# Where the diagonal blocks of B are built in a four-layer sequence kernel with a two-way state-space layer

## The reference, cut to what matters

```python
dbc = einsum('bse,re->bsr', u, Wdbc)
dlt, Bm, Cm = split(dbc, [R, R + N], axis=-1)          # R = 64, N = 16
delta = softplus(einsum('bsr,er->bse', dlt, Wdt) + bdt)
dA = exp(delta[..., None] * A)
dBu = delta[..., None] * Bm[:, :, None, :] * u[..., None]
h = dA_t * h + dBu_t                                    # per time step
y = einsum('ben,bn->be', h, C_t)
```

## Time and profile before

| what | value |
|---|---|
| median of 3 runs | 6139.45 us (6117.95 to 6150.0) |
| profiled execution | 6128.12 us, span 6126.3 us |
| input pass | about 2757 to 3141 us of the span |
| scans | about 3141 to the end |
| PE busy | 5604.4 us, 91% |
| DVE busy | 4365.8 us, 71% |
| ACT busy | 2988.3 us, 49% |
| POOL busy | 2959.0 us, 48% |
| mean granted TensorE clock | 0.977 of full speed |

### The profile page before, as it was taken

One profiled execution on the slowest core, in us unless ns is written; L12 is line 12 of the kernel. 1 busy time (PEld: TensorE's weight loads), 2 busy tenths in 40 slices (PEclk: granted clock), 3 DMA queues, 4 the chain that ended last, 5 costly groups with the idle time before them and its releaser, 6 DMA issues. The chain is left out here.

```text
span 6126.3 us, 136499 instructions
## 1 busy us (share of the span) xinstructions
PE 5604.4 (91%) x58464; PEld 3147.5 (51%) x58464; DVE 4365.8 (71%) x5868; ACT 2988.3 (49%) x4999; POOL 2959.0 (48%) x953
## 2 busy tenths in 40 slices
PE   8899979997999989977989999999999999999998
PEld 2455545554455545543445555555555555555555
DVE  1165545554455555557549999999999999999996
ACT  0022212221455555551137666666666666666664
POOL 0000100000000000004349989899899998989997
PEclk9999989998999999988999999999999999999999
DMA  5200120001000000004431101111111111101110
GB/s 209 80 16 31 38 73 16 31 33 59 18 8 17 22 20 17 8 15 156 154 122 47 61 19 57 60 56 61 41 50 50 57 64 50 65 23 57 62 47 31
DMA packets 142972, 321.72 MB, mean 53 GB/s; under 512 B 25769, under 2 KB 27050, under 8 KB 132154
## 3 DMA queue, kind: packets, MB, share of 16 engines
q1 hardware_dynamic: 142402, 313.39, 14.7%
HBM read 238.46 MB, written 74.89 MB: 51 GB/s over the span
## 5 line engine op out<-in xcount | busy, mean ns | idle before, releaser
L1847 POOL TENSOR_TENSOR sc_state<-sc_state,sc_c_rows 128x2048 f32<-128x2048 f32 x512 | 2374.6, 4643 | 282.6 <-DVE sc_state L2154 268.2
L2154 DVE TENSOR_TENSOR_SCAN sc_state<-sc_decay,wide 128x512 f32<-128x512 f32 x2048 | 2346.4, 1200 | 100.1 <-PE wide L2013 95.5
L1938 ACT ACTIVATE sc_decay<-sc_delta,sc_neg_a 128x512 f32<-128x512 f32 x2048 | 1455.6, 720 | 813.2 <-DVE sc_state L2154 808.4
L2013 PEld LDWEIGHTS wide<-sc_diag,sc_du_t 64*64 64x64 f32 x32768 | 971.4, 133 | 688.1 <-issue 450.8
L2013 PE MATMUL wide<-sc_diag,sc_du_t 64*64 64x128 f32 x32768 | 1172.4, 273 | 136.6 <-DVE sc_state L2154 136.6
L2030 PE MATMUL wide<-sc_state,sc_half 64*64 64x512 f32 x8192 | 1077.1, 592 | 11.4 <-POOL sc_state L1847 11.4
L1328 DVE CUSTOM_DVE_ANT_0 l_prob<-wide,l_mask_add 128x512 f32<-128x512 f32 x512 | 340.1, 683 | 286.8 <-PE wide L1198 286.8
L1987 PE MATMUL wide<-sc_xn_t,sc_w_z 128*128 128x512 f32 x1024 | 510.0, 621 | 1.2 <-DMA sc_xn_t<-xn_d 1.2
L1113 ACT ACTIVATE l_prob<-l_prob,l_s_max 128x512 f32<-128x512 f32 x512 | 366.1, 716 | 229.3 <-DVE l_s_max L1328 228.9
L460 PE MATMUL wide<-l_w,l_xn_t 128*128 128x512 f32 x1024 | 445.1, 592 | 1.7 <-PEq L84 1.7
L1209 PE MATMUL wide<-l_ident,l_prob 128*128 128x128 f32 x2048 | 293.6, 281 | 65.3 <-DVE l_prob_t L1337 38.2
(11 more groups left out here) (197 smaller groups left out, 6605.0 us busy)
## 6 DMA issues: line engine op xcount, KB each, us to landing
sc_c_rows<-c_d SPq DMA_DIRECT2D x64, 1024.0 KB, 4.8
sc_w_z<-wz_tiles SPq DMA_DIRECT2D x128, 256.0 KB, 2.7
x<-l_out SPq DMA_DIRECT2D x24, 1024.0 KB, 4.2
l_x<-x SPq DMA_DIRECT2D x16, 1024.0 KB, 5.9
mx_d<-fr_mx SPq DMA_DIRECT2D x16, 1024.0 KB, 4.2
sc_mx<-mx_d SPq DMA_DIRECT2D x64, 256.0 KB, 2.7
pro_w_mod<-in_mod_w SPq DMA_DIRECT2D x6, 2048.0 KB, 8.4
l_w<-in_att_w SPq DMA_DIRECT2D x12, 1024.0 KB, 11.9
```

The costliest lines, as they stand in the source:

```text
L1847: pool.tensor_tensor(state[quad % STATES][:, :, :], state[quad % STATES][:, :, :], c_rows[(r * 4 + q) % ROWS][:, :, :], ALU.mult).then_inc ...
L1938: act.activation(decay[step % DECAYS][:, :], delta[slot % 2][:, :], ACT.Exp, scale=neg_a[:, s, m, n:n + 1]).then_inc(decay_ready, 1)
L2013: last = pe.matmul(to[cols_to, k, :, :], du_t[slot % 2][rows, k, cols_to], diag[rows, c, k, :, :], start=True, stop=True)
L2154: dve.tensor_tensor_scan(state[quad % STATES][:, step % 4, order], decay[step % DECAYS][:, order], pair[:, i, order], 0.0, ALU.mult, ALU.a ...
```

## The change

In the input pass the B product takes its time steps with a stride of four, so that b_tm already has the layout which the scans want, and b_tm has two buffers. GpSimd builds the diagonals of both sweeps there, into two buffers of 16 KB per partition, one for each sweep. Its builds of batch b stand in later iterations: the forward ones after the residual of batch b+1, the backward ones after the first 1/sqrt of batch b+2. SP stores them (2 MB for each sweep) to diag_d at the end of the iteration of the following batch. b_d is gone. In the scans GpSimd builds nothing; SP loads the eight chunks of `diag` (256 KB each) one by one as TensorE finishes with the old ones, and TensorE waits on one semaphore per chunk.

```diff
@@ front_layer @@
+        b_tm = [sb(f"b_tm{j}", [P, TT, 2, N]) for j in two]
+        half = sb("half", [P, 64])
+        diag = [sb(f"diag{s}", [P, 8, 4, 64, 2]) for s in two]
+                def store_diag(b, s):
+                    sp.wait_ge(diag_built[s], 8 * (b + 1))
+                    sp.dma_start(d["diag_d"][b, s], diag[s][:, :, :, :, :].rearrange("p c k j n -> p (c k j n)")
+                                 ).then_inc(diag_stored[s], 16)
...
-                    sp.wait_ge(b_drained, b + 1)
-                    sp.dma_start(d["b_d"][b].rearrange("(t p) n -> p t n", p=P),
-                                 b_tm[:, :, :, :].rearrange("p t s n -> p t (s n)")).then_inc(b_stored, 16)
                     for h in range(2):
                         sp.wait_ge(mx_ready, b * ET + h * 4 + 4)
                         sp.dma_start(d["mx_d"][b, h * 4:(h + 1) * 4].rearrange("m p t -> p m t"),
                                      mx[:, h * 4:(h + 1) * 4, :]).then_inc(mx_stored, 16)
+                    if b >= 1:
+                        for s in range(2):
+                            store_diag(b - 1, s)
+                for s in range(2):
+                    store_diag(B - 1, s)
...
+                def build(b, s):
+                    if b == 0:
+                        pool.wait_ge(half_loaded, 16)
+                    pool.wait_ge(b_drained, b + 1)
+                    if b >= 1:
+                        pool.wait_ge(diag_stored[s], b * 16)
+                    for c in range(8):
+                        pool.tensor_tensor(diag[s][:, c, :, :, :],
+                                           b_tm[b % 2][:, :, s, 2 * c:2 * c + 2].unsqueeze(2).broadcast_to([P, 4, 64, 2]),
+                                           half[:, :].unsqueeze(1).unsqueeze(3).broadcast_to([P, 4, 64, 2]), ALU.mult
+                                           ).then_inc(diag_built[s], 1)
                 for b in range(B):
                     rsqrt(b, mv, rstd, mv_ready, var_ready, rstd_ready)
+                    if b >= 2:
+                        build(b - 2, 1)
                     rsqrt(b, mv2, rstd2, mv2_ready, var2_ready, rstd2_ready)
                     residual(b)
+                    if b >= 1:
+                        build(b - 1, 0)
+                build(B - 2, 1)
+                build(B - 1, 0)
+                build(B - 1, 1)
...
-                                             xn_t[j][:, k, t * P:(t + 1) * P], w_dbc[:, :, k, R + N:R + 2 * N],
+                                             xn_t[j][:, k, t::4], w_dbc[:, :, k, R + N:R + 2 * N],
...
-                    if b >= 1:
-                        dve.wait_ge(b_stored, b * 16)
+                    if b >= 2:
+                        dve.wait_ge(diag_built[0], 8 * (b - 1))
+                        dve.wait_ge(diag_built[1], 8 * (b - 1))
@@ scan_layer @@
+                def load_diag(r, c):
+                    sp.dma_start(diag[:, c, :, :, :].rearrange("p k j n -> p (k j n)"),
+                                 d["diag_d"][r // 2, r % 2][:, c * 512:(c + 1) * 512]).then_inc(diag_loaded[c], 16)
...
                 load_xn(0)
+                for c in range(8):
+                    load_diag(0, c)
                 for quad in range(4):
                     load_c(quad)
...
                     if m == 7 and r + 1 < 2 * B:
-                        for q in range(1, 4):
-                            sp.wait_ge(weighted, 4 * slot + q)
-                            load_c(4 * (r + 1) + q)
+                        for c in range(8):
+                            sp.wait_ge(dbu_full, 4 * (8 * slot + c + 1))
+                            load_diag(r + 1, c)
+                            if c in (5, 7):
+                                q = (c - 3) // 2
+                                sp.wait_ge(weighted, 4 * slot + q)
+                                load_c(4 * (r + 1) + q)
+                        sp.wait_ge(weighted, 4 * slot + 3)
+                        load_c(4 * (r + 1) + 3)
...
-                    if m == 7 and r + 1 < 2 * B:
-                        build(r + 1, 2 * q)
-                        build(r + 1, 2 * q + 1)
...
-                        pe.wait_ge(diag_ready, r * 8 + c + 1)
+                        pe.wait_ge(diag_loaded[c], (r + 1) * 16)
```

More of the change, by code:

```diff
@@ L1412, in front_layer @@
         dbc = [sb(f"dbc{s}", [R + N, T]) for s in two]
-        b_tm = sb("b_tm", [P, TT, 2, N])
+        b_tm = [sb(f"b_tm{j}", [P, TT, 2, N]) for j in two]
+        half = sb("half", [P, 64])
+        diag = [sb(f"diag{s}", [P, 8, 4, 64, 2]) for s in two]
         stats = sb("stats", [P, TT, 6])
@@ L1430, in front_layer @@
         xn_stored, mx_stored, resid_stored = sem("xn_stored"), sem("mx_stored"), sem("resid_stored")
-        dbc_stored, b_stored = sem("dbc_stored"), sem("b_stored")
+        dbc_stored, half_loaded = sem("dbc_stored"), sem("half_loaded")
+        diag_built, diag_stored = [sem(f"diag_built{s}") for s in two], [sem(f"diag_stored{s}") for s in two]
         with nc.Block() as block:
@@ L1453, in _ @@
                 sp.dma_start(wx[:, :, :], d["wxT"].rearrange("(k p) n -> p k n", p=P)).then_inc(wx_loaded, 16)
+                sp.dma_start(half[:, :], d["half_ident"]).then_inc(half_loaded, 16)
                 load(1)
+                def store_diag(b, s):
+                    sp.wait_ge(diag_built[s], 8 * (b + 1))
+                    sp.dma_start(d["diag_d"][b, s], diag[s][:, :, :, :, :].rearrange("p c k j n -> p (c k j n)")
+                                 ).then_inc(diag_stored[s], 16)
                 for b in range(B):
@@ L1477, in _ @@
                 sp.wait_ge(dbc_stored, B * 64)
-                sp.wait_ge(b_stored, B * 16)
+                for s in range(2):
+                    sp.wait_ge(diag_stored[s], B * 16)
                 sp.wait_ge(mx_stored, B * 32)
@@ L1582, in drains @@
                     dve.wait_ge(b_full, b + 1)
-                    if b >= 1:
-                        dve.wait_ge(b_stored, b * 16)
-                    dve.tensor_tensor(b_tm[:, :, :, :], banks[4][:, 0:TT * 32].rearrange("p (t s n) -> p t s n", t=TT, s=2),
+                    if b >= 2:
+                        dve.wait_ge(diag_built[0], 8 * (b - 1))
+                        dve.wait_ge(diag_built[1], 8 * (b - 1))
+                    dve.tensor_tensor(b_tm[b % 2][:, :, :, :], banks[4][:, 0:TT * 32].rearrange("p (t s n) -> p t s n", t=TT, s=2),
                                       b_bias[:, :, R + N:R + 2 * N].unsqueeze(1).broadcast_to([P, TT, 2, N]), ALU.add
@@ L1655, in scan_layer @@
         dlt = [sb(f"dlt{i}", [P, T]) for i in two]
-        b_tm = [sb(f"b_tm{i}", [P, 4, N]) for i in two]
         diag = sb("diag", [P, 8, 4, 64, 2])
@@ L1681, in scan_layer @@
         w_z_loaded = [sem(f"w_z_loaded{i}") for i in range(WZ)]
-        dlt_loaded, b_loaded = [sem(f"dlt_loaded{i}") for i in two], [sem(f"b_loaded{i}") for i in two]
+        dlt_loaded, diag_loaded = [sem(f"dlt_loaded{i}") for i in two], [sem(f"diag_loaded{c}") for c in range(8)]
         c_loaded = [sem(f"c_loaded{i}") for i in range(ROWS)]
@@ L1685, in scan_layer @@
         gate_loaded, out_stored = sem("gate_loaded"), [sem(f"out_stored{i}") for i in two]
-        diag_ready, dl_full, soft_ready, delta_ready = sem("diag_ready"), sem("dl_full"), sem("soft_ready"), sem("delta_ready")
+        dl_full, soft_ready, delta_ready = sem("dl_full"), sem("soft_ready"), sem("delta_ready")
         z_full, z_direct, du_ready, turned, du_t_ready = sem("z_full"), sem("z_direct"), sem("du_ready"), sem("turned"), sem("du_t_ready")
@@ L1707, in load_set @@
                         sp.dma_start(dlt[r % 2][i * R:(i + 1) * R, :], d["dlt_d"][b, s]).then_inc(dlt_loaded[r % 2], 16)
-                        sp.dma_start(b_tm[r % 2][i * 64:(i + 1) * 64, :, :],
-                                     d["b_d"][b, i * 256:(i + 1) * 256, s * N:(s + 1) * N].rearrange("(j k) n -> j k n", k=4)
-                                     ).then_inc(b_loaded[r % 2], 16)
+                def load_diag(r, c):
+                    sp.dma_start(diag[:, c, :, :, :].rearrange("p k j n -> p (k j n)"),
+                                 d["diag_d"][r // 2, r % 2][:, c * 512:(c + 1) * 512]).then_inc(diag_loaded[c], 16)
                 def load_c(quad):
@@ L1754, in _ @@
                             sp.wait_ge(dl_full, 16 * r)
-                            sp.wait_ge(diag_ready, 8 * r)
                         load_set(r + 1)
@@ L1806, in _ @@
                 pool.wait_ge(const_loaded, 4 * 16)
[L1808 to L1817, removed]
                 def gating(slot):
@@ L1835, in output @@
                                        ).then_inc(out_ready, 1)
-                for c in range(8):
-                    build(0, c)
                 for quad in range(QUADS):
@@ L2190, in program @@
                             ("resid_d", [B, T, D]), ("xn_d", [B, P, DT * T]), ("mx_d", [B, ET, P, T]),
```

(2 more changed lines are left out.)

## The result

The changed kernel takes 6190.5 us (median of 4 runs, 6187.8 to 6193.1), the one before 6139.1 (4 runs, 6118.0 to 6150.0). The ratio is 1.009, with a 95% interval of 1.007 to 1.011: slower, by some 51 us. The profiled executions are 6191.0 and 6128.1 us, 63 us apart. The forecast was 6158, "no change".

| stretch | before | after | difference |
|---|---|---|---|
| up to the first xn_t store | 2799.5 | 2797.5 | −2 |
| first to last xn_t store | 297.5 | 355.0 | +57.5 |
| last xn_t store to last mx store | 38.9 | 45.3 | +6.3 |
| to the end of the pass (last store landed) | 4.2 | 31.7 | +27.5 |
| to the first du of the scans | 18.0 | 18.8 | +0.8 |

A forecast was written before the change was run, and what follows sets the result against it. TensorE was taken as fullest in the scans and as setting the input pass's pace. From 6128.1 us, −30 (scans), +1 (their start), +30 (input-pass loop) and +28 (tail) gave 6157, stated as 6158; range 6120 to 6190 for 8 in 10.

The forecast's parts named there:

- no change: Whole kernel: within 0.5%, 6109 to 6170 us; chance 0.54, of which 0.34 the forecast itself and 0.2 hidden builds.
- the loop: Input pass: xn_t store to that two batches later, through diagonal stores, builds and normalisation, 95.3 us against TensorE's 85.2; +30 us.
- normalisation: Input pass: VectorE to the second mean and variance, 9.4 us now, held by reverse builds of 8.4, so 17.8.
- The prediction's other sum: Input pass, VectorE's normalisation beside the builds: a handover at every build, each stretched by 0.5 us, gives 12.4 + 5.0 = 17.4.
- The tail: After the last mx store: diagonal stores and batch 7's builds without cover, 32.5 us against 4.2, +28 us.
- The scans: Without builds at sweep changes GpSimd is on time and VectorE's addition L2126 is no longer held: 30 us won.
- the upper bound of 32: Scans: the most the removed builds could win, in us, if the first boundary between sweeps gives something too.
- The start of the scans: First diagonal loads go ahead of the second w_z, which lands 3.5 us late, partly hidden: +1 us (0 to 4).
- The loads of diagonals: Scan boundaries: eight 256 KB loads hidden by 20 us of cover, cost 0; rival of TensorE waiting, 6170 to 6220, chance 0.04.
- holds that stay in the scans: Rival: L2126's three long holds stay and only the four small ones go, 6181 us; chance 0.30, slower stores included.
- slower stores: Input pass: diagonal stores at 8.4 us per 2 MB lengthen pairs and tail by 2 to 4 us each, 6168.
- slower: Whole kernel: scans keep their holds (0.30) or loads replace builds as the wait (0.04), together chance 0.34.

The follow-up runs named there:

- the first experiment: The changed kernel, with the input pass's B product reading its weights from 128 neighbouring columns of xn_t instead of every fourth: 6164.5 us.
- Keeping the builds apart: The changed kernel with neighbouring columns as B product weights and the backward builds moved behind the residual, away from VectorE's normalisation: 6146.0 us.
- the early stores: The changed kernel, with SP issuing a batch's two diagonal stores before the two mx stores instead of behind them: 6150.0 us.
- the two experiments on it: Stride of four taken out of the changed kernel's B product, 6164.5 us; the stride alone put into the kernel before, 6170.8 us.

## Why the prediction was wrong

**The step that failed** is the last sentence of the part on the input pass: "The strided weights of the B product have the form of the scans' transposes of du and cost nothing I can price above 1 us per batch." They cost 3.8 us of matmuls and 2.6 us of lower clock per batch, 6.4 together; against the kernel before 5.2 are left of it (47.8 and 42.6 us), in part because three of the batches before have their own, shorter fall of the clock. The evidence was a row of another instruction form: a transpose's weight load, 211 ns at a stride of four. The bound from the nearest row was not drawn either: 211 against 141 ns already said that a stride of four slows a load by half, and the B product is 32 loads behind each other with matmuls of only 32 columns between them (3.65 us for all 32 when packed). The stride alone is worth 43.6 us (2791.5 to 3126.6 and 44.9 more, against 297.5 and 38.9); beside the loop it adds 26 (the first experiment), since TensorE's longer batches lie in part under the loop's waits. With those 26 the forecast of 6158 would have read 6184.

**The loop was right in kind and nearly in size.** It was taken apart step by step, pair 3 to 5: 45.3 instead of 38.9 (the stride), 11.3 to the landed store instead of 9.0 (10.8 from the issue of the store; xn_t and the residual are issued 2.4 us behind it, and where nothing follows so soon the store lands in 8.7), builds 8.1 for 8.4, normalisation 15.7 for 17.8, xn 14.6, transposes and drain about 4.6 for 3.8. The prediction's other sum, with VectorE let in at every build, had given 17.4; the trace shows exactly that order, and the term is still shorter because the handovers stretch a build from 1.05 to 1.2 and 1.5 us and not by 0.5 each (eight in 10.16 us instead of 12.4). Keeping the builds apart brings the normalisation back to 9.4 us and the pair 3 to 5 from 98.1 to 91.7; the early stores bring the pairs down to TensorE's own pace. So the mechanism is shown and not only argued. That the pairs without the stride come so near 95.3 is partly luck: there too the landing is longer and the normalisation shorter than in the sum. And the sum left out what the waits do to the clock. Without the stride L1582 takes 9.43 us in batch 7, behind a wait of 11 us and at a granted clock of 0.70, instead of 7.09, and batch 3, from which the pair of 98.1 starts, loses the same 2.2 us. Batch 0 loses them too (9.34 us, at 0.69), by chance, for the kernel before has the same wait in front of it and 7.09 us. From the first xn_t store to the last mx store that kernel takes 39 us more than the kernel before, and 30 were forecast.

**The tail was right**: 32.5 forecast, 31.7 measured; the last 2 MB land in 6.3 us, 6.6 forecast.

**The scans were right**, 30 forecast and 33.6 measured. The first change of sweeps, which only the upper bound of 32 held, gave 1.9 us, and the sweep behind the second 1.2 us more than its 8.6.

**The start of the scans was mis-sized**, 1 us forecast and 7.3 measured. The second w_z landed 29.7 us after the end of the pass instead of 22.4, so it came 7.3 us later and not 3.5. TensorE stood still for 5.9 us in front of its product, and the four matmuls L2012 then took 3.78 us, at a granted clock of 0.50, instead of 1.98. Most of the wait had been taken as hidden behind the scans.

**The loads of diagonals never bound**: TensorE waits for none at a sweep's change, as forecast.

**The range** ended at 6190.0, half a microsecond below the median. Its upper end stood for holds that stay in the scans, which did not happen, and for slower stores; the stride had no part in it. That the result lies so near it is chance. The chance of "slower" was 0.34; "no change" at 0.54 rested on the missing term.

**The comparison's own noise** was seen rightly. The run with strided transposes, whose scans are those of the kernel before, happened to have five holds of 7.6 us and more and took 6142 us; the profile of before had three and took 6128: 7 us for a hold. The kernel before spreads over 6102 to 6154 us in 27 runs, each kernel without the holds over 3 to 9 us.

## What to carry to other kernels

Price an index expression like an instruction: a stride of four float32 in a matmul's weights was paid at every load, one of two hardly, and the row that prices it must be of the same form. When builds or stores are moved into a pass with slack, follow who waits for the buffer they free: here the place of a store in SP's order cost 40 us, where 32 MB of stores and 128 builds cost little but a tail of 14 us in the same pass. A busy neighbour costs where it is late, so spreading its work evenly can be worth as much as moving it away.

## What the runs showed of the hardware

A weight load of 128 float32 columns takes 192 ns packed, 196 ns at a distance of 8 bytes and 329 ns at 16 bytes; a transpose's takes 141 to 151, and 209 at 16 bytes. So the cost comes as a step between 8 and 16 bytes and not as a slope. In each batch of the kernels with the stride the granted clock fell to 0.50 for 6.8 us, from 5.2 to 5.7 us after the start of the 32 slow matmuls on, in a TensorE that was not idle there; in three of eight batches of the kernel before it fell for 3.4 us behind the 32 packed loads. That the stride makes the fall longer and regular is shown by the two experiments on it, what sets it off stays open. VectorE's addition with two SBUF inputs (L1640) is held by GpSimd builds like the single-input form (L1636), and each instruction let in stretches the next build, by 0.2 us for the one and 0.4 for the other. When GpSimd's next instruction is ready at once, VectorE sometimes isn't let in at all, and whether it is differs from one change of sweeps to the next and from trace to trace: of the same scans, the kernel before has three holds of 7.6 us and more, the one with stride two has two, the one with strided transposes five.
